# Attention and FP4 feed-forward block on one core: where the maxima stand between the bursts of the value product

## The reference

```python
# embeddings (8, 1024, 512), w_qkv (512, 1536), 16 heads of 32
def attn(embeddings, w_qkv):
    result = (embeddings @ w_qkv).reshape(b, s, 3, 16, 32)
    q, k, v = (jnp.transpose(result[:, :, i], (0, 2, 1, 3)) for i in range(3))
    scores = jnp.einsum('bnqd,bnkd->bnqk', q, k) / jnp.sqrt(jnp.float32(512))
    ctx = jnp.einsum('bnqk,bnkd->bnqd', jax.nn.softmax(scores, axis=-1), v)
    return jnp.transpose(ctx, (0, 2, 1, 3)).reshape(b, s, h)

# ffn: fp4_linear quantises x and w blockwise (16) to the FP4 grid, then multiplies
def ffn(x, w_gate, w_up, w_down):
    h = silu(fp4_linear(x, w_gate)) * fp4_linear(x, w_up)
    return fp4_linear(h, w_down)

x = layernorm(x + attn(x, w_qkv))
x = layernorm(x + ffn(x, w_gate, w_up, w_down))
```

## Time and profile before

| | us |
|---|---|
| median of three runs | 3924.18 (3923.32 to 3925.02) |
| the profiled execution | 3922.93 |
| its span, first to last instruction | 3921.3 |
| PE busy | 3744.5 (95%) |
| DVE busy | 3024.0 (77%) |
| POOL busy | 2232.0 (57%) |
| ACT busy | 1709.7 (44%) |

### The profile page before, as it was taken

One profiled execution on the slowest core, in us unless ns is written; L12 is line 12 of the kernel. 1 busy time (PEld: TensorE's weight loads), 2 busy tenths in 40 slices (PEclk: granted clock), 3 DMA queues, 4 the chain that ended last, 5 costly groups with the idle time before them and its releaser, 6 DMA issues. The chain is left out here.

```text
span 3921.3 us, 61535 instructions
## 1 busy us (share of the span) xinstructions
PE 3744.5 (95%) x22853; PEld 1727.3 (44%) x22853; DVE 3024.0 (77%) x5075; ACT 1709.7 (44%) x3085; POOL 2232.0 (57%) x1427
## 2 busy tenths in 40 slices
PE   3599999999999999999999999999999999999999
PEld 2244454344544355443544445434454334544354
DVE  9876787678876688667877678767887668866787
ACT  2166423663246532555226542366424553255522
POOL 1298624984268832787229862398425883278722
PEclk9699999999999999999999999999999999999999
DMA  5211101011011110111101110101101111010110
GB/s 169 81 36 34 55 21 37 17 43 48 25 31 32 35 47 20 43 27 35 47 20 39 31 57 20 39 17 42 49 22 33 30 37 46 20 42 25 31 52 22
DMA packets 106565, 152.53 MB, mean 39 GB/s; under 512 B 28176, under 2 KB 55568, under 8 KB 106128
## 3 DMA queue, kind: packets, MB, share of 16 engines
q1 hardware_dynamic: 106256, 148.49, 12.2%
HBM read 76.28 MB, written 19.66 MB: 24 GB/s over the span
## 5 line engine op out<-in xcount | busy, mean ns | idle before, releaser
L604 DVE TENSOR_REDUCE mx<-R 128x1 f32<-128x512 f32 x2080 | 1316.9, 683 | 536.1 <-PE R L698 533.1
L1265 ACT ACTIVATE arena<-SC 128x512 f32<-128x512 f32 x1360 | 755.6, 603 | 407.9 <-PE SC L1531 279.2
L1606 PE MATMUL SC<-wgu,split 128*128 128x512 f16 (+1 forms) x3456 | 714.5, 361 | 0.0
L1176 POOL TENSOR_TENSOR arena<-arena,sc_h 128x704 f32<-128x704 bf16 (+1 forms) x144 | 178.0, 1250 | 606.1 <-DVE arena L528 606.1
L1150 POOL TENSOR_TENSOR wd<-wd,arena 128x1024 f32<-128x1024 f32 x212 | 494.2, 2358 | 44.5 <-ACT arena L1265 44.5
L1606 PEld LDWEIGHTS SC<-wgu,split 128*128 128x128 f16 x3456 | 338.3, 98 | 331.4
L1265 ACT ACTIVATE wd<-SC 128x512 f32<-128x512 f32 x688 | 389.8, 603 | 211.8 <-PE SC L1531 149.1
L1307 ACT ACTIVATE arena<-SC,gain 128x512 f32<-128x512 f32 (+1 forms) x192 | 125.1, 651 | 810.2 <-PE R L1606 411.9
L678 PE MATMUL R<-xT,wqkv 128*128 128x512 bf16 x1632 | 421.5, 380 | 19.5 <-DVE xT L591 13.1
L698 PE MATMUL R<-ks_even,qs_even 96*128 96x512 bf16 x1056 | 395.0, 389 | 27.6 <-DVE mx L604 7.8
L698 PE MATMUL R<-arena 96*128 96x512 bf16 x1024 | 374.0, 382 | 13.2 <-DVE xT L591 8.2
(11 more groups left out here) (138 smaller groups left out, 5496.6 us busy)
## 6 DMA issues: line engine op xcount, KB each, us to landing
x<-n_L_attn_embeddings_dram SPq DMA_DIRECT2D x136, 256.0 KB, 2.8
wd<-wd_kept SPq DMA_DIRECT2D x32, 512.0 KB, 5.4
out_dram<-x SPq DMA_DIRECT2D x64, 256.0 KB, 2.0
ks_even<-split SPq DMA_DIRECT2D x204, 64.0 KB, 2.0
qs_even<-split SPq DMA_DIRECT2D x408, 32.0 KB, 1.8
arena<-split SPq DMA_DIRECT2D x192, 64.0 KB, 2.0
arena<-split SPq DMA_DIRECT2D x384, 32.0 KB, 1.8
wd<-wd_kept SPq DMA_DIRECT2D x16, 384.0 KB, 7.2
```

The lines of the kernel that those rows point to most:

```text
L604: nc.vector.reduce_max(mx[:, j:j + 1], ring_of(ring, job)[:, :], AX_X).then_inc(max_done, 1)
L1176: nc.gpsimd.tensor_tensor(blocks_of(q_h[:, cols]), blocks_of(r_h[:, cols]), spread(sc_h[:, c], c.stop - c.start), ALU.mult).then_inc(qh_do ...
L1265: nc.scalar.activation(probs_of(s)[:, hd, :], SC[e % SLOTS][:, :], ACT.Exp, scale=SCALE).then_inc(exp_done, 1)
L1606: last = nc.tensor.matmul(GU[kk % 2][which][:, 0:w], xhT[i % 2][:, part_x * KH + k, :], wgu[:, part_w * KH + k, which * I + first:which * ...
```

## The change

The numbers of maxima in steps 1 to 4 become 4, 6, 4, 6 where they were 5 each. In steps 2, 4 and 6 one maximum stands in front of the first score, none between the first and the second, and up to three directly in front of the burst (in step 2 in front of the sum). Quarters of projections in these steps stand behind the burst. In step 0 one more maximum stands in front of the burst and none at the end. In odd steps the second quarter moves in front of a maximum, and the step ends with a score or a quarter.

```diff
@@ -86,8 +86,8 @@
 
 QUARTERS = 4
 POOL_SUMS = [TILES - 2] * (UNITS - 1) + [TILES // 2]
-MAX_STEPS = (5, 5, 5, 5, 5, 4, 3, 0)
-MAX_STEPS_LAST = (5, 5, 5, 5, 5, 4, 1, 2)
+MAX_STEPS = (5, 4, 6, 4, 6, 4, 3, 0)
+MAX_STEPS_LAST = (5, 4, 6, 4, 6, 4, 1, 2)
 MADE = (((1, (4, 5)), (1, 1, 1, 1, 1, 1, 1, 1)), ((2, (0, 1)), (1, 1, 1, 1, 1, 1, 1, 1)),
         ((2, (2, 3, 4)), (2, 2, 2, 1, 1, 1, 2, 1)), ((2, (5,)), (3, (0, 1)), (2, 1, 1, 2, 1, 2, 2, 1)),
         ((3, (2, 3, 4)), (2, 2, 2, 1, 1, 1, 2, 1)), ((3, (5,)), (4, (0,)), (4, 0, 0, 0, 0, 1, 1, 2)),
@@ -139,8 +139,10 @@
     total = [("sum", u - 1, 0)] if u > 0 and t == SUM_STEP else []
     neg = [("neg", u + 1, 0)] if t == TILES - 1 and not ends else []
     if t == 0:
-        return of_batch(b, (m[0:1] + q[0:1] + m[1:2], m[2:3], [], m[3:4] + q[1:2], other, m[4:5] + q[2:] + m[5:]))
-    return of_batch(b, ([], m[0:1] + q[0:1], m[1:2] + total, neg + m[2:3] + other, m[3:4] + q[1:2], m[4:5] + q[2:] + m[5:]))
+        return of_batch(b, (m[0:1] + q[0:1] + m[1:3], m[3:4], [], m[4:5] + q[1:2], other, q[2:]))
+    if t % 2 == 0:
+        return of_batch(b, (m[0:1], [], m[1:4] + total, neg + other + q[0:1], m[4:5] + q[1:2], m[5:6] + q[2:]))
+    return of_batch(b, ([], m[0:1] + q[0:1], m[1:2], neg + q[1:2] + m[2:3] + other, m[3:4], q[2:]))
 
 
 def first_jobs(b):
```

## The result

The changed kernel takes 3996.28 us (median of four runs, 3996.05 to 3998.35) against 3924.2: 1.0186 times as long, interval 1.0174 to 1.0198. It is slower by 72 us; the forecast was 4006, within 3950 to 4035.

The account below looks back on a forecast made before the run. TensorE was taken to wait for PSUM banks that VectorE gives back late. Terms 5.94 + 0.76 + 0.69 + 2.76 + 0.15 make 10.3 us a batch, +82 over eight batches: from 3924.2 to about 4006 us, range 3950 to 4035.

Parts of the forecast that it names:

- (a): First burst to sum, units 1 to 7: the last maxima and the sum wait for banks, 5.94 us a batch more.
- (b): Unit 0, which has no sum: its first burst needs the tenth maximum's bank, 0.76 us a batch more.
- (c): Sum to third burst: in units 2 and 4 the tenth maximum waits behind the seventh; 0.69 us a batch more overall.
- (d): Third to fourth burst: in units 2 and 4 V's first quarter waits for a later low half; 2.76 us a batch overall.
- (e): The rest: moved maxima cost nothing, unit 6's wait for low halves; 0.15 us a batch for all.
- 99 us of loss before: TensorE's true loss in 374 load waits on VectorE: 144.0 us less 0.12 us normal gap each.
- The sign that it named: Waits of R matmuls on maxima and low halves larger by 60 to 90 us.
- the walk: Hand walk through program order with trace durations, giving TensorE's waits for banks: 82 us more; 63% chance.
- Burst filled: Faster rival: three maxima before a burst fill VectorE's idle time there, half of 99 us goes: 3874 us, 6%.
- Pairs of scores: Rival, even steps: each second adjacent score waits 0.28 us for ScalarE, 54 us on top: 4060 us, 8%.
- The smaller loss: Rival: banks and late low halves counted twice; without (d) and half of (a), 36 us more: 3960 us, 12%.
- The banks are the limit whatever the order: Rival: maxima side by side gain nothing, only waits in front of the sum cost, 26 us: 3950 us, 8%.

Follow-up runs that it names:

- quarters46: The changed kernel with the first quarter of steps 4 and 6 back between the first two scores: 3964.95 us.
- apart: The changed kernel with a maximum between the first two scores of steps 2, 4 and 6, leaving two directly in front of the burst: 3999.24 us.
- places: The changed kernel with the old numbers of maxima, the fifth of an odd step at its end: 4039.31 us.
- counts: The kernel before with the new numbers of maxima and the old arrangement inside the steps: 3944.41 us.
- half_before: The kernel before with VectorE reducing only the first 256 of each maximum's 512 columns: 3863.38 us.

## Why the prediction was right

Per batch, in us; measured are the medians over eight batches, with what moved past a burst (a quarter 0.65, a maximum 0.22) set off:

```
                                 forecast   measured
(a) burst 1 to sum, units 1-7      5.94       4.54
(b) unit 0, first burst            0.76       0.75
(c) sum to third burst             0.69       0.59
(d) third to fourth burst          2.76       3.30
(e) the rest                       0.15       0.29
sum                               10.30       9.47
```

The span grew by 73.1, or 9.1 a batch; the forecast was 82. (The medians add up to a little more, as some units of before were longer than their median.)

**What bounds it.** Right. The count of instructions is the same, the loss is waits of R matmuls on VectorE, and with shorter reductions most of it goes. But the forecast's 99 us of loss before is too high. It took 0.12 us off each of the 374 waits of loads and counted the rest as TensorE's; by the starts of the matmuls it is some 34, and shorter reductions, which also hasten low halves' banks, took 60 off. The sum of (a) to (e) doesn't use the 99; the price of the faster rival and the lower bound of the sum do. The sign that it named, 60 to 90 us more of R waits on maxima and low halves, needs the same care: by the rows of the loads they grew by 119 us, by the starts of the matmuls by some 64.

**(a)** is the term that was mis-sized. "Unit 1 (...) the sum stands at 6.85": it stands at 8.49 - 1.86 = 6.63. "It stands at 7.29" in unit 2: 8.95 - 1.86 = 7.09. In both the walk's own release of the bank fits (in unit 2 the seventh maximum starts at 6.38, and 6.38 + 0.71 = 7.09), and I had put 0.20 on top between release and sum. The sum starts as the bank comes free. Seven sums of 0.20 are the 1.4 of (a) and 11 us in all; (d) and (e) were too low by 0.7 a batch, so the total came out closer than its largest term. In unit 6 it was 0.88 and in unit 7 1.01, each 0.2 under the walk.

**(b), (c)** fit within 0.1.

**(d)** had the right mechanism and was 0.5 low. Units 2 and 4: 1.04 and 1.06 for 0.96 (the forecast's own two waits, 0.66 and 0.35, make 1.01; unit 2 of the second batch has 0.67 and 0.31). Unit 3: -0.54 for -0.63. Unit 5: 0.70 for 0.55. quarters46 shows the cause in units 2 and 4 by taking it away.

**(e)** was called nothing but for 0.15. In unit 6 the way from the transposed maxima to the first burst grew by 0.27 beyond the moved maximum, at the quarters that need the transposed x; their waits went from 13.1 to 16.6 us in all. The scores of units 3 and 5 didn't wait for the later q1 stack: these units' first intervals grew by the moved maximum alone (1.75 to 1.96).

**The rivals.** *Burst filled:* VectorE filled 1.21 us of the burst, where it had filled 0.82, and still idled 1.43 us behind it. *Pairs of scores:* the waits came (+42 us in the two rows), and apart showed that taking them away gains nothing. The forecast's reason, that exponentials are ready in time, was nearly right for the matmuls (9 us more of late starts) and wrong for the loads. The rival's price, 0.28 us a wait, was read from the loads. *The smaller loss* (without (d), half of (a)): (d) measured 3.30 and (a) 4.54, more than half, and quarters46 undid most of (d) in units 2 and 4. *The banks are the limit whatever the order:* "whatever the order" is refuted. With the same four banks orders from 3897 to 4039 us were found, and 45 of the 72 us go with shorter reductions. That 27 us are left there and its price was 26 is chance: it priced the waits in front of the sums alone, and in the 27 are also those on low halves and of scores. Which is not to say that the banks play no part: a maximum waits because its bank isn't free, and no run had more than four. The rule from the Trainium skill (Perfetto Trace Analysis, Optimization Strategy) that consistent bubbles can mean too little PSUM was therefore not put to the test.

**VectorE's pace.** Five reductions in a row take 3.07 us after, (3.07 - 0.68) / 4 = 0.60 each, as before. The rule of the Trainium skill (VectorE: DVE Perf Modes, the section on the TRN2 errata), 0.66 by its cycles, would have had the sums later than forecast; they came earlier. That they came earlier is the 0.20 of (a) and no measure of the pace.

**A gap of the forecast:** it said that from burst to burst ten maxima stand before and after (between the third and fourth it is nine, in both), and left it there. That the new numbers are what keeps it so in the new order, where the old ones would give eleven, and that they cost 22 us in the old order, it didn't see.

## What to carry to other kernels

Where tiles go to a slower reader through banks in a fixed turn, count for each stretch between two long operations how many tiles stand in it and how many the reader can have done since it last ran dry: beyond the number of free banks a further tile can cost the reader's time (0.60 from after to places), not the writer's (0.22). Spread the tiles: saved up for the end they run out of banks (after), and so do four in close turn right behind the long operation (counts). Look which tile a late by-product (here the low half) stands behind. A wait of the weight loads is not yet a wait of the matmuls: compare the matmuls' starts. And a wait row that grows is a cause only if the time falls with it: take it away once before believing it.

## What was not expected

- A wait of 42 us in all on exponentials could be taken away without a gain in time (3999.24 against 3996.28); by the matmuls' starts it had hardly been 5.
- Reducing 256 of 512 columns takes VectorE 421 ns a tile instead of 683 (before), by the costliest groups of half_before and before; 0.62 of the time for half the columns. Each has its view here, half_before first:

```profile
L604 DVE TENSOR_REDUCE mx<-R 128x1 f32<-128x256 f32 x2080 | 837.2, 421 | 907.7 <-PE R L698 901.2
```

```profile
L604 DVE TENSOR_REDUCE mx<-R 128x1 f32<-128x512 f32 x2080 | 1316.9, 683 | 536.1 <-PE R L698 533.1
```

- Two parts of one edit with prices of +22 and +117 us made +72 together.
